# First attention: scores computed in pairs over alternating row halves, and half of the softmax sum moved to GpSimd

## What is computed

```python
xn = _layernorm(x, ln_gamma, ln_beta)
q = (xn @ w_q).reshape(B, SQ, NUM_HEADS, DIM_HEAD)
k, v = jnp.split(context @ w_kv, 2, axis=-1)          # each as 16 heads of 64
scores = jnp.einsum('bqhd,bkhd->bhqk', q * SCALE, k)
attn = jax.nn.softmax(scores, axis=-1)
out = jnp.einsum('bhqk,bkhd->bqhd', attn, v).reshape(B, SQ, INNER)
out = out @ w_out + b_out
```

## Time and profile before

| | us |
|---|---|
| median of 3 runs | 334.52 |
| lowest and highest run | 334.09, 336.31 |
| the profiled execution, its span from first to last instruction | 334.5 |
| first scores start in it | 41.08 |
| last scores (step 31) start in it | 122.67 |

### The profile page before, as it was taken

How to read it: one execution, slowest core, us unless ns; L and a number is a source line. 1 busy time by engine, 2 the same in 40 slices (tenths; PEclk the granted TensorE clock), 3 DMA queues, 4 the chain that set the end, 5 groups by cost and what they waited for, 6 DMA issues and landing times.

```text
span 334.5 us, 6100 instructions
## 1 busy us (share of the span) xinstructions
PE 317.7 (95%) x2241; PEld 273.2 (82%) x2241; DVE 195.4 (58%) x586; ACT 161.1 (48%) x278; POOL 71.7 (21%) x92
## 2 busy tenths in 40 slices
PE   1999999999999998899996999999999999999995
PEld 1578877888888887798984997889999888998994
DVE  3779768977998986246868483942434162112112
ACT  2483447765664445323353647627533553534530
POOL 1174015667734332010045410100010000000000
PEclk9999999999999999899999999999999999999999
DMA  7799000000000000430000000000000001000001
GB/s 211 233 307 185 0 0 2 3 4 11 19 0 2 0 2 3 145 139 1 0 2 1 2 0 2 0 0 2 3 1 2 0 0 33 0 2 2 0 0 34
DMA packets 10013, 11.31 MB, mean 34 GB/s; under 512 B 1049, under 2 KB 6833, under 8 KB 9984
## 3 DMA queue, kind: packets, MB, share of 16 engines
q1 hardware_dynamic: 9600, 10.55, 10.4%
q0 software_dynamic: 384, 0.36, 1.0%
HBM read 10.39 MB, written 0.52 MB: 33 GB/s over the span
## 4 chain that ended last, share of the span: by engine, by line
PE 82%; DVE 11%; issue 2%; POOL 2%; DMA 2%; ACT 0%; SPq 0%; DVEq 0%
PE bank L1024 28%; PE bank L875 9%; PE bank L876 9%; PE bank L877 8%; PE bank L822 8%; PE bank L831 4%; PE bank L860 4%; DVE xhat_sb L654 3%; PE bank L846 3%; DMA ctx_tok_sb<-in_ctx 2%; PE bank L910 2%; DVE sum_sb L593 2%; DVE negmax_sb L585 1%; PE bank L943 1%; PE bank L957 1%
## 5 line engine op out<-in xcount | busy, mean ns | idle before, releaser
L557 ACT ACTIVATE hT_sb<-bank,cols_sb 128x512 f32<-128x512 f32 x104 | 69.9, 687 | 82.7 <-PE bank L877 81.9
L799 DVE SCALAR_TENSOR_TENSOR x_sb<-bank,wts_sb,x_sb 128x128 f32<-128x128 f32 x128 | 36.0, 344 | 84.2 <-PE bank L1024 84.2
L1024 PEld LDWEIGHTS bank<-we_sb,hT_sb 128*128 128x128 f32 x576 | 66.5, 192 | 1.1
L1024 PE MATMUL bank<-we_sb,hT_sb 128*128 128x128 f32 x576 | 67.2, 275 | 0.0
L462 POOL TENSOR_TENSOR p_sb<-p_sb,recip_sb 128x480 f32<-128x480 f32 x32 | 31.6, 986 | 58.1 <-DVE recip_sb L596 58.1
L822 PE MATMUL bank<-kT_sb,qT_sb 64*128 64x120 f32 x256 | 36.8, 284 | 0.0
L822 PEld LDWEIGHTS bank<-kT_sb,qT_sb 64*128 64x128 f32 x256 | 30.8, 187 | 5.8 <-issue 5.2
L1024 PEld LDWEIGHTS bank<-w_sb,hT_sb 128*128 128x128 f32 x256 | 31.8, 198 | 1.6 <-issue 0.9
L1024 PE MATMUL bank<-w_sb,hT_sb 128*128 128x128 f32 x256 | 32.5, 282 | 0.0
L875 PE MATMUL bank<-xnT_lo_sb,we_hi_sb 128*128 128x512 f32 x72 | 30.4, 422 | 0.0
L876 PE MATMUL bank<-xnT_hi_sb,we_hi_sb 128*128 128x512 f32 x72 | 28.5, 396 | 0.0
(11 more groups left out here) (159 smaller groups left out, 476.0 us busy)
## 6 DMA issues: line engine op xcount, KB each, us to landing
we_sb<-in_L_ffn_We SPq DMA_DIRECT2D x1, 2048.0 KB, 8.3
w_kv_sb<-in_L_xattn_w_kv SPq DMA_DIRECT2D x2, 512.0 KB, 6.6
w_sb<-in_L_ffn_w SPq DMA_DIRECT2D x1, 1024.0 KB, 10.5
x_sb<-in_x SPq DMA_DIRECT2D x1, 512.0 KB, 7.2
w_q_sb<-in_L_xattn_w_q SPq DMA_DIRECT2D x1, 512.0 KB, 8.7
w_out_sb<-in_L_xattn_w_out SPq DMA_DIRECT2D x1, 512.0 KB, 7.9
we_sb<-in_L_ffn_Ws SPq DMA_DIRECT2D x2, 256.0 KB, 10.3
ctx_tok_sb<-in_ctx SPq DMA_DIRECT2D x2, 240.0 KB, 4.8
```

The lines of the kernel that those rows point to most:

```text
L557: nc.scalar.activation(hT[:, u % 2, c, :], ps(item)[:, :], ACT.Relu if n == 1 else ACT.Silu, bias=cols[:, col:col + 1]).then_inc(read(item ...
L799: last = nc.vector.scalar_tensor_tensor(out=x[:, b, :], in0=ps(item)[:, C * i:C * (i + 1)], scalar=w, in1=x[:, b, :], op0=ALU.mult, op1=AL ...
L1024: last = nc.tensor.matmul(dst[:, C * i:C * (i + 1)], hT[:, slot, c, 128 * i:128 * (i + 1)], wb[:, e, c, :], start=(c == 0), stop=(c == chu ...
```

## The change

The scores of steps i and i + 1 are computed together at attend(i), for even i: the passes of the two steps, which lie in different row halves, alternate, and fill two banks. The four score banks are 0, 1, 5 and 7; the value products keep bank 4 alone, and the late queries have banks 4 and 6 instead of 4, 5 and 7. As there are no scores at attend 1, the late queries are bundled in 4 and 4 chunks behind attend 0 and 1.

GpSimd adds keys 0 to 59 and 60 to 119 of the exponentials of a step into `half0` (128 rows, 4 heads, 60 sums), and VectorE sums those 60 instead of 120. GpSimd's multiplication comes one item later than before, behind the addition of the step after it.

```diff
-    late_queries = ((0, 1, 2), (3, 4), (5, 6, 7))
+    late_queries = ((0, 1, 2, 3), (4, 5, 6, 7))
...
+    S0_BANKS = (0, 1, 5, 7)
...
-            spare = (4, 5, 7) if item[0] == "q0" else (0, 1) if item[0] == "up" else (7,)
+            spare = (4, 6) if item[0] == "q0" else (0, 1) if item[0] == "up" else (6,)
...
-            if i < STEPS:
-                plan(("s0", i), i % 2)
+            if i < STEPS and i % 2 == 0:
+                plan(("s0", i), S0_BANKS[i % 4])
+                plan(("s0", i + 1), S0_BANKS[i % 4 + 1])
...
-                plan(("o0", i - LPV), 4 + (i - LPV) // 2 % 2)
+                plan(("o0", i - LPV), 4)
...
+        half0 = xnT[:, HALF:HALF + HG * SK].rearrange("p (r h k) -> p r h k", r=2, h=HG)
...
-                elif item[0] == "attend" and 0 <= item[1] - 1 < STEPS:
-
+                elif item[0] == "attend" and 0 <= item[1] - 1 <= STEPS:
                     j = item[1] - 1
-                    pool.wait_ge(recip_ready, j + 1)
-                    nc.gpsimd.tensor_tensor(p0[j % 4], p0[j % 4], recip0[:, j % 2, :].unsqueeze(2)
-                                            .broadcast_to([128, HG, SK]), ALU.mult).then_inc(probs_ready, 1)
-                    if 8 <= j < len(late) + 4:
-                        load(*late[j - 4])
+                    if j < STEPS:
+                        pool.wait_ge(exps0_ready, j + 1)
+                        if j >= 2:
+                            pool.wait_ge(recip_ready, j - 1)
+                        nc.gpsimd.tensor_tensor(half0[:, j % 2], p0[j % 4][:, :, 0:SK // 2], p0[j % 4][:, :, SK // 2:SK],
+                                                ALU.add).then_inc(halves_ready, 1)
+                    j = item[1] - 2
+                    if j >= 0:
+                        pool.wait_ge(recip_ready, j + 1)
+                        nc.gpsimd.tensor_tensor(p0[j % 4], p0[j % 4], recip0[:, j % 2, :].unsqueeze(2)
+                                                .broadcast_to([128, HG, SK]), ALU.mult).then_inc(probs_ready, 1)
+                        if 8 <= j < len(late) + 4:
+                            load(*late[j - 4])
...
-                    dve.wait_ge(exps0_ready, j + 1)
-                    link(nc.vector.tensor_reduce(sum0[:, j % 2, :], p0[j % 4], AX, ALU.add))
+                    dve.wait_ge(halves_ready, j + 1)
+                    link(nc.vector.tensor_reduce(sum0[:, j % 2, :], half0[:, j % 2], AX, ALU.add))
...
-                if i < STEPS:
-                    key = ("s0", i)
+                if i < STEPS and i % 2 == 0:
                     b, g = i // GROUPS, i % GROUPS
-                    dst = open_bank(pe, key)
-                    r0 = DH * (g % 2)
+                    dst = [open_bank(pe, ("s0", i)), open_bank(pe, ("s0", i + 1))]
...
-                        last = nc.tensor.matmul(dst[:, SK * j:SK * (j + 1)], qT[r0:r0 + DH, c, 128 * b:128 * (b + 1)],
-                                                kT[r0:r0 + DH, c, SK * b:SK * (b + 1)], start=True, stop=True)
-                    last.then_inc(full(key), 1)
+                        for odd in range(2):
+                            r0 = DH * odd
+                            last = nc.tensor.matmul(dst[odd][:, SK * j:SK * (j + 1)],
+                                                    qT[r0:r0 + DH, c, 128 * b:128 * (b + 1)],
+                                                    kT[r0:r0 + DH, c, SK * b:SK * (b + 1)], start=True, stop=True)
+                            if j == HG - 1:
+                                last.then_inc(full(("s0", i + odd)), 1)
```

More of the change, by code:

```diff
@@ L328, in flamingo_kernel @@
         exps0_ready = sem("exps0_ready")
+        halves_ready = sem("halves_ready")
         recip_ready = sem("recip_ready")
```

## The result

The changed kernel takes 344.37 us (median of 4 runs, 341.91 to 346.15) beside 334.38 us for the kernel before: a ratio of 1.0277, 95% interval 1.0233 to 1.032. It is slower by 10.0 us between the medians, 9.3 us by the ratio, where 331.6 was forecast and 338.5 was the top of the range. The profiled execution is the fastest of the four, the 341.91 us run, with a span of 340.1.

The account below looks back on a forecast made before the run. TensorE was taken to set the pace from step 8 to about 20, with VectorE sharing it afterwards. 334.5 less 3.8 at maximum 31 plus 0.8 taken back gave 331.5, stated as 331.6 us, range 328.5 to 338.5.

Parts of the forecast that it names:

- the stage from 8 to 20: Attention from maximum 8 at 63.8 to maximum 20 at 93.5, with GpSimd the bound at 4.98 us per two loaded steps.
- The pair of scores: TensorE's scores of two steps: sixteen passes at 0.056 us plus 0.18, 1.08 us in place of 2 x 1.08.
- The addition: GpSimd's new addition of 240 elements per step: taken as 0.70 us, between bounds of 0.49 and 0.99.
- The reduction: VectorE's sum in each step: 0.41 us instead of 0.642, making a step 1.77 us.
- The wait in the first query bundle: Start of the attention: query chunk 2 waits for a bank until ScalarE's first copy, costing 1.25 us.
- Maximum 8: VectorE's row maximum of step 8: starts at 63.8 us, where before it was at 62.10.
- VectorE's own work from 20 to 31: Last stage of the attention: eleven steps of 19.5 us and extras of about 6.7, together 26.2.
- loads queue: Rival: weight loads of the two row halves don't overlap, a pair takes 1.96 us, total 337.1; chance 0.22.
- I take back 0.8 us: Allowance on the total for VectorE instructions slowed beside GpSimd's additions and for falls of TensorE's clock: 0.8 us.
- the rival of four falls: TensorE's clock falls four times in the attention stage, 1.2 us each, total 336.4; chance 0.07.
- where the loop is longer I add 0.4: Steps 20 to 31: 0.4 us added to VectorE's 26.2 for where the loop between engines is longer.
- The profiled span, 334.5, is the median of the runs, so nothing is added.: Base of the total: the profiled span of the kernel before, 334.5 us, taken as its median run time.

Follow-up runs that it names:

- e23: Changed kernel without GpSimd's addition, with four query banks and idle TensorE matmuls (eight in step 4, three in steps 5, 9, 13 and so on): 332.98 us, 0.9918.
- e22: Changed kernel with first queries over four banks and idle TensorE matmuls (eight in step 4, four in steps 5, 9, 13 and so on): 335.04 us, 1.0005.
- e21: Changed kernel with only idle TensorE matmuls added (eight in step 4, four in steps 5, 9, 13 and so on): 338.28 us, 1.0101.
- e1: Changed kernel without GpSimd's addition: scores in pairs, VectorE sums all 120 keys, GpSimd multiplies as before: 334.56 us, 1.0013.
- e2: Kernel before with GpSimd's addition, VectorE's sum over 60 and the later multiplication, scores unpaired: 340.95 us, 1.0216.
- e3: Changed kernel with ScalarE taking a step's exponential before its copies of earlier steps: 348.54 us, 1.041.
- e7: Changed kernel with the eight late loads issued by SyncE instead of GpSimd: 347.89 us, 1.0418.
- e9: Changed kernel with the eight passes of the even step ahead of the odd step's eight, not alternating: 350.45 us, 1.0431.
- e17: Changed kernel with GpSimd's addition done twice in a row: 359.65 us, 1.0763.

## Why the prediction was wrong

With full clock up to maximum 31 in four of the profiles, the terms can be read off stage by stage. Times in us; the first row is where maximum 8 starts, the next two are from maximum to maximum, the fourth is what is left of the span.

| | before | pairs (e23) | + addition (e22) | + query wait (e21) | + clock falls (after) | forecast |
|---|---|---|---|---|---|---|
| to maximum 8 | 62.10 | 60.73 | 61.82 | 63.80 | 66.05 | 63.8 |
| 8 to 20 | 32.30 | 28.69 | 31.58 | 31.59 | 33.24 | 29.7 |
| 20 to 31 | 29.46 | 29.35 | 30.39 | 30.39 | 30.46 | 26.6 |
| maximum 31 at | 123.86 | 118.77 | 123.79 | 125.78 | 129.75 | 120.1 |
| behind it | 210.64 | 212.53 | 208.61 | 208.82 | 210.35 | as before |

At maximum 31 the pairs (with the filling and free query banks) bring 5.1 us, the addition costs 5.0, the query wait 2.0 and the clock 4.0: together 5.9 later. The step from e23 to e22 also moves the multiplication behind the next addition and makes the filling one matmul longer; no run has them apart. In the ratios of the runs, from 0.9918 by way of 1.0005 and 1.0101 to 1.0277, it is 2.7 us gained, then 2.9, 3.2 and 5.9 lost. Each ratio is known to 1.2 to 1.6 us either way, so a step between two of them to about 2. They differ from the profiles mostly by what happens behind the attention, where the falls of the clock come in some executions and not in others (last row).

The forecast has maximum 31 at 120.1, and it came at 129.75. The clock has 4.0 of these 9.65 us, the stage from 20 to 31 has 3.8 (30.39 for 26.6), and the stage from 8 to 20 has 1.9 (31.59 for 29.7).

**Right.** The pair of scores: 1.16 us, forecast 1.08. The addition: 0.69, forecast 0.70. The reduction: 0.39, forecast 0.41. The wait in the first query bundle, forecast 1.25: TensorE stands idle 0.93 at 45.03, maximum 2 is at 51.13 (forecast 50.9). Maximum 8 at full clock is at 63.80 in e21, and 63.8 was forecast; that it fits so closely is luck, since e21's filling is not in the sum. VectorE's own work from 20 to 31: forecast 26.2, measured 25.38. The rival "loads queue" fell by the 1.16 us.

**Wrong: the clock.** The step "I take back 0.8 us", with the rival of four falls at a chance of 0.07. This is the largest term: 4.0 us in the profiles, 5.9 of 9.3 by the ratios. The argument against it was full clock in this stage. But those rows are of a TensorE that has no gaps in it; the change is what makes the gaps. I had written down that TensorE "now has gaps of 1 to 2 us", and that the one fall of the trace came behind such gaps, and still priced them with that single fall, at 1.2 us. In the profile the stage has two falls, which together cost 4.0.

**Wrong: the stage from 20 to 31.** The step "where the loop is longer I add 0.4". VectorE's busy time was right; its idle time wasn't. Busy time by stretches from maximum 20 to maximum 31, of the kernel before, of e23_pair_gap_small and of e21_gap_small (columns as above):

```profile
94.40:123.86 29.46, 29.32 (x268) 25.53 (x268) 27.18 (x62) 15.26 (x28) 11.55 (x12) 1.00 0.01 1
```

```profile
89.42:118.77 29.35, 25.40 (x280) 22.11 (x282) 27.10 (x61) 14.59 (x26) 11.55 (x12) 1.00 0.00 1
```

```profile
95.39:125.78 30.39, 26.80 (x294) 23.37 (x294) 25.38 (x61) 15.19 (x27) 19.74 (x24) 1.00 0.00 1
```

VectorE is idle 2.3 us before, 2.3 with pairs alone and 5.0 with the addition. With pairs alone this stage takes as long as before, 29.35 (29.34 in e1, without filling): TensorE's relief (29.32 to 25.40 busy) is worth nothing there, so VectorE set the pace already. The addition takes 1.8 us of VectorE's work away and gives back 2.7 of waiting. VectorE's waits in that stretch of e21_gap_small (in total, times, longest us):

```profile
DVE x_sb L613 <- PE bank L876: 2.0, 3, 0.9
DVE logits_sb L707 <- PE bank L959: 1.2, 1, 1.2
```

The 1.2 us are there with pairs alone too. The 2.0 us are not: they are for the projection, which TensorE issues behind transposes. Ahead of the longest of the three waits, 0.90 us, TensorE's timeline has

```profile
121.21 0.62 PE L847 MATMUL bank<-ident_sb,p_sb 128*120 128x128 f32 x4 [1.48 <-POOL p_sb L473]
121.67 1.95 PE L876 MATMUL bank<-w_out_sb,w_kv_sb 128*128 128x128 f32 x16
```

The wait for `p_sb` is passed on to whoever needs the next thing in TensorE's queue. My sum held VectorE against its own work, and took the rest of the loop for 0.4.

**Too small: the stage from 8 to 20.** Forecast 29.7, at full clock 31.59. Of that stretch GpSimd is busy 29.31 us in e21_gap_small, 93%:

```profile
63.80:95.39 31.59, 28.18 (x317) 24.70 (x318) 24.58 (x58) 18.73 (x37) 29.31 (x42) 1.00 0.04 9
```

GpSimd is as loaded as forecast, and the 2.3 us that are left are waits. Addition 9 starts 4.7 us behind maximum 8 (forecast 4.4) and addition 17 comes 20.45 behind it (forecast 19.9). The other 1.1 us come after that. There VectorE waits for the projection again, a wait that the sum doesn't have:

```profile
90.98 0.35 DVE L613 SCALAR_TENSOR_TENSOR x_sb<-bank,gA_sb,x_sb 128x128 f32<-128x128 f32 x1 [0.70 <-PE bank L876]
```

In this stage the addition costs 2.9 us (28.69 to 31.58). So the addition was mis-sized not in its 0.69 us, but in where it lies: 32 of them cost 5.0 us at full clock, where I had counted a gain of 0.24 us a step for VectorE. e2 has nearly the same without pairs, 5.3 us.

**Misread, without effect: the base.** "The profiled span, 334.5, is the median of the runs, so nothing is added." In every run a time is its span and about 1.8 us more (341.91 and 340.1 here). The span of 334.5 belongs to the 336.31 us run, and the median run, 334.52 us, was another with a shorter span. The two numbers agree by luck, so the sum started from the right time.

The sign came out wrong because three errors had the same direction. They are one omission: a wait put into TensorE's queue was priced by its own length, and not by what stands behind it and what the clock does about it.

**What stays open.** Why e23_pair_gap_small has a fall of the clock behind the attention in all ten runs (mean clock 0.987 to 0.995), while five of ten of e22_banks_small are at 1.00. In the profiles it is 3.9 us (212.53 against 208.61); filling there wasn't tried. Nor do the runs separate how much of the losses of e3, e7, e9 and e17 is clock and how much is the way, since no filling was run with them.

## What to carry to other kernels

Relieving the engine that is 95% busy opens gaps in it, and on TensorE a gap can cost twice: once as a wait, and again when the clock falls behind it. So before work is taken from TensorE, ask if the next engine is already within a few per cent of its pace (VectorE was, from step 20 on), and fill the gaps that are left, with idle matmuls cut to the measured wait: four at the right places gained 6 us, eight in every second step lost about 3. Work moved to an engine that is idle most of the time is not free if it is put between two engines that hand a buffer round: count its whole length in each turn of that way, and then what is queued behind whoever waits.

## What the runs showed of the hardware

- Sixteen fp32 passes of 64 rows and 120 columns take 1.16 us in alternating row halves and 1.70 in two runs of eight; in the kernel before, with other pieces between the two halves, they took 2 x 1.08.
- Behind waits of 2.20 and 0.84 us TensorE's pieces take 1.98 and 2.07 us in place of 1.09 and 1.16, nearly double, as at 1.2 GHz in place of 2.4. With most of these waits filled (e21) the granted clock is 1.00 in the whole stage.
- An fp32 matmul with a 128-column identity shows as two passes, 0.12 us each at full clock (eight matmuls, x16, 1.95 us); an fp32 transpose of 128 by 120 shows as one (x4, 0.62 us).
- VectorE's split (L589) takes 1.35 us beside GpSimd's multiplication, which itself takes 1.17 in place of 0.99:

```profile
116.11 1.35 DVE L589 TENSOR_TENSOR xnT_lo_sb<-xnT_sb,xnT_hi_sb 128x512 fp32r<-128x512 f32 x1
```

```profile
115.74 1.17 POOL L473 TENSOR_TENSOR p_sb<-p_sb,recip_sb 128x480 f32<-128x480 f32 x1
```

These are of e21_gap_small; in the kernel before the same instruction of VectorE took 0.69 us, without GpSimd beside it. The Trainium skill (SBUF — State Buffer, Who interferes with whom) says that a VectorE instruction with two inputs in SBUF contends with a GpSimd instruction that reads SBUF, over a port pair that is locked exclusively. Both rows agree in direction: when the split starts, the multiplication has 0.80 us to go, and the split takes 0.66 longer.
